# Twelve middle label slabs of a DLRM tower moved from VectorE to GpSimd and ScalarE

## The reference, cut to what matters

```python
score = exp((x @ w_a + b_a) @ w_b); p = softmax(where(mask == 0, PAD, score))
q     = einsum('bne,bn->be', x, p)                 # for two heads
h     = concat(q1, q2) @ w5 + b5
f7    = (h[:, iu] * h[:, ju] * g) @ w7 + b7
out8  = concat(h @ w6 + b6, f7) @ w8 + b8
z     = einsum('bu,bku->bk', out8, label_embedding)   # 1024 x 200 label rows of 300
y     = relu(relu(concat(z, ctx) @ W_top1 + b1) @ W_top2 + b2) @ W_top3
```

## Time and profile before

| what | value |
|---|---|
| median of 3 runs | 1833.36 us (1830.81 to 1834.02) |
| the profiled execution's own time | 1835.06 us |
| its span, first to last instruction | 1833.3 us |
| PE, DVE, ACT, POOL busy | 92%, 91%, 55%, 31% of the span |
| DMA, mean rate | 306 GB/s, 561.69 MB |
| mean granted clock of TensorE | 0.971 |

### The profile page before, as it was taken

The page is one execution under the profiler, slowest core; times in us unless marked ns, Lnnn a source line. Parts: engine busy times, 40 slices in busy tenths (PEclk is TensorE's granted clock), DMA queues, the critical chain, the costliest instruction groups (busy, mean ns, idle before and its releaser), DMA issues.

```text
span 1833.3 us, 25723 instructions
## 1 busy us (share of the span) xinstructions
PE 1686.3 (92%) x6972; PEld 1244.5 (68%) x6972; DVE 1661.9 (91%) x5847; ACT 1011.6 (55%) x3167; POOL 570.6 (31%) x419
## 2 busy tenths in 40 slices
PE   2888999999999999999999999999998999997754
PEld 1555667777767777777777777777775777775533
DVE  5988979989999889999999999899999788967777
ACT  3776693674466643466654664446753444354535
POOL 7778807828300135500077018600000000000044
PEclk8899999999999999999999999999999999999977
DMA  8388846847988689889868766998749999989987
GB/s 277 108 275 307 308 164 229 323 164 289 381 303 319 235 334 349 342 342 351 297 224 333 279 250 202 377 418 320 255 138 376 420 413 369 416 311 419 418 324 292
DMA packets 98222, 561.69 MB, mean 306 GB/s; under 512 B 16799, under 2 KB 17158, under 8 KB 72478
## 3 DMA queue, kind: packets, MB, share of 16 engines
q1 hardware_dynamic: 77917, 498.35, 70.5%
q0 software_dynamic: 19424, 61.65, 10.6%
q10 hardware_dynamic: 736, 0.05, 0.0%
HBM read 559.98 MB, written 0.00 MB: 305 GB/s over the span
## 4 chain that ended last, share of the span: by engine, by line
PE 42%; DVE 34%; DMA 10%; issue 6%; POOL 5%; ACT 2%; SPq 0%; DVEq 0%; POOLq 0%; ACTq 0%
PE acc L1132 37%; DVE qa L744 13%; DVE junk L700 12%; DVE prod L854 8%; DMA w_sb<-in_w 7%; POOL x L639 3%; DMA lab<-in_labels 2%; POOL lab L639 2%; ACT waste L1275 1%; PE coarse L938 1%; PE acc L985 1%; PE misc L950 1%; PE acc L988 1%; ACT prod L1380 1%; PE acc L970 1%
## 5 line engine op out<-in xcount | busy, mean ns | idle before, releaser
L1132 PE MATMUL acc<-w_sb,prod 128*128 128x300 f32 (+2 forms) x5648 | 1511.5, 421 | 59.8 <-DMA w_sb<-in_w 35.8
L1132 PEld LDWEIGHTS acc<-w_sb,prod 128*128 128x128 f32 (+2 forms) x5648 | 1052.8, 192 | 424.1 <-issue 48.6
L1380 ACT ACTIVATE prod<-prod,g_all 128x256 f32<-128x256 f32 (+4 forms) x1615 | 675.1, 470 | 475.9 <-DVE prod L854 471.2
L639 POOL DMA_INDIRECT x<-in_tbl,ids_sb x368 | 488.4, 1327 | 644.7 <-DVE qa L744 534.2
L854 DVE TENSOR_TENSOR prod<-fine,coarse 128x1280 f32<-128x1280 f32 (+3 forms) x320 | 419.5, 1316 | 93.1 <-PE coarse L938 72.3
L700 DVE SCALAR_TENSOR_TENSOR junk<-lab,heads 128x300 bf16<-128x300 f32 x1208 | 477.7, 462 | 10.9 <-DMA lab<-in_labels 9.6
L700 DVE SCALAR_TENSOR_TENSOR junk<-x,heads 128x300 bf16<-128x300 f32 x1128 | 445.4, 462 | 24.0 <-DMA x<-in_tbl,ids_sb 22.0
L744 DVE SCALAR_TENSOR_TENSOR qa<-x,ex,qa 128x300 f32<-128x300 f32 x612 | 275.7, 526 | 0.1
L674 POOL TENSOR_TENSOR x<-x,out 128x2400 f32<-128x2400 f32 x5 | 26.2, 5254 | 592.8 <-ACT out L1235 583.7
L1275 ACT ACTIVATE waste<-x 128x300 bf16<-128x300 f32 x368 | 161.7, 440 | 26.2 <-DMA x<-in_tbl,ids_sb 24.5
L1203 ACT ACTIVATE fine<-misc 128x512 f32<-128x512 f32 (+3 forms) x70 | 37.5, 535 | 116.9 <-PE misc L950 88.4
(11 more groups left out here) (123 smaller groups left out, 571.0 us busy)
## 6 DMA issues: line engine op xcount, KB each, us to landing
w_sb<-in_w SPq DMA_DIRECT2D x320, 750.0 KB, 6.7
lab<-in_labels SPq DMA_DIRECT2D x146, 1200.0 KB, 9.0
x<-in_labels SPq DMA_DIRECT2D x54, 1200.0 KB, 10.7
x<-in_tbl,ids_sb POOLq DMA_INDIRECT x368, 5.5
w_sb<-in_w SPq DMA_DIRECT2D x5, 450.0 KB, 3.3
prod<-in_v_i SPq DMA_DIRECT2D x1, 710.0 KB, 4.4
prod<-in_v_j SPq DMA_DIRECT2D x1, 710.0 KB, 5.8
w_sb<-in_w SPq DMA_DIRECT2D x1, 703.1 KB
```

The source lines that it names most:

```text
L639: pool.indirect_dma_start(out=row_of(t, n), out_offset=None, in_=tables[n], in_offset=bass.IndirectOffsetOnAxis(ap=ids_sb[:, t % IDS_RING, ...
L1132: last = pe.matmul(acc[:, t % 3, 0:EMB], prod[0:rows, u % RING, m, t % 2 * P:(t % 2 + 1) * P], w7_sb[0:rows, u % W7_RING, m * EMB:(m + 1) ...
L1380: act.activation(chunk, chunk, ACT.Copy, scale=g_all[0:rows, pair:pair + 1]).then_inc(chunk_ready, 1)
```

## The change

During the attention of tiles 4 to 7 the planner may give a label slab to POOL and ACT instead of DVE. It does so when a slab would be DVE's next item, the next item of `rest` is the `mask` of a tile t over 3, the slab is none of the first one or the last four of its label tile, the model says that all rows of t have landed, at least two `dots` items of t after the next are left, and POOL's last such multiplication is 60 (6 us by the model's clock) ago. DVE then takes the next item in its place at once. ACT's eight sums get a tick each from three units later on, in one sequence with the `sum_abs` rows, so that these move back; the slot is held to the last of the sums. POOL multiplies these slabs after the last gather of tile t and before the first of t + 1.

Followed through, the planner's arithmetic with its constants gives twelve such slabs: 11, 12, 14, 15 (labels of tile 0, beside the attention of tile 4; first sums at ticks 470, 493, 506, 524), 40, 43, 44 (tile 1, beside tile 5; 690, 698, 731), 69 (tile 2, beside tile 6; 895) and 84, 87, 88, 90 (tile 3, beside tile 7; 1050, 1058, 1091, 1104). All of DVE's other items keep their cost, but many change their unit. The `mask` of tile 4 stays at unit 111, that of tile 5 moves from 161 to 153, that of 6 stays at 191, that of 7 moves from 232 to 227. Up to the last unit of two tiles DVE ends its slabs at unit 280 instead of 283, tile 6's labels begin at unit 288 as before, and one slab more, 173, is done between the units (19 slabs of the tail are 18). `y` of tiles 1 and 3 comes 30 and 35 ticks later, that of 2 and 4 comes 30 and 15 ticks earlier.

The diff, cut to its core:

```diff
+POOL_COST = 60
@@ plan() @@
+    by_pool, pool_end = {}, 0
@@
         elif not (item and at <= now):
+            slab = None
             now = min(when for when in (1e9 if held else due, at, slab_at) if when > now)
             continue
+        if item == slab and c < TOTAL and rest and rest[0][0] == "mask" and 0 < slab[2] < SLABS - 4:
+            t = rest[0][1]
+            if (t > 3 and landed.get((t, HALVES - 1), 1e9) <= now and dots and dots[0][1] == t
+                    and dots[0][2] < HALVES - 2 and pool_end <= now):
+                pool_end = now + POOL_COST
+                for k in range(SLAB):
+                    abs_tick = max(abs_tick + 1, (u + 3) * FINE)
+                    pool_ticks.setdefault(abs_tick, []).append(("sum", nslab, k))
+                by_pool[nslab] = t
+                slab_end.append(now + (abs_tick - u * FINE) * UNIT[2] // FINE)
+                continue
@@ after plan() @@
+BEFORE, ITEMS, TAIL, POOL_TICKS, LOADS, SWITCH, MIDDLE = plan()
+SUMMED = {n: max(tick for tick, work in POOL_TICKS.items() if ("sum", n, SLAB - 1) in work) for n in MIDDLE}
-BY_POOL = [(TILES - 1) * SLABS + s for s in range(1, SLABS, 3)]
+BY_LAST = [(TILES - 1) * SLABS + s for s in range(1, SLABS, 3)]
+BY_POOL = list(MIDDLE) + BY_LAST
@@ schedule() @@
-        tick = (LABELLED.get(t, TOTAL) + 1) * FINE + 2
+        tick = max([(LABELLED.get(t, TOTAL) + 1) * FINE + 2] + [SUMMED[n] + 2 for n in MIDDLE if n // SLABS == t])
@@ POOL @@
+            def multiply(n):
+                pool.wait_ge(out8_ready, n // SLABS + 1)
+                slot, loads = slab_slot(n)
+                pool.wait_ge(slab_loaded[slot], 16 * loads)
+                row8 = out8[:, n // SLABS % OUT8, :]
+                row8 = bass.AP(tensor=row8.tensor, offset=row8.offset,
+                               ap=[list(row8.ap[0]), [0, SLAB], [1, EMB]])
+                pool.tensor_tensor(slab_place(slot), slab_place(slot), row8, ALU.mult).then_inc(multiplied, 1)
@@ POOL, for t in range(2, TILES), behind the gathers of t @@
+                for n in MIDDLE:
+                    if MIDDLE[n] == t:
+                        multiply(n)
@@ PE, turn_z @@
+                if sums_up_to(t):
+                    pe.wait_ge(sums_done, sums_up_to(t))
@@ ACT @@
+            def sum_row(slab, k):
+                t, column = slab // SLABS, slab % SLABS * SLAB + k
+                if k == 0:
+                    act.wait_ge(multiplied, BY_POOL.index(slab) + 1)
+                    if t >= Z_RING:
+                        act.wait_ge(y_stored, 16 * (t - Z_RING + 1))
+                slot, _ = slab_slot(slab)
+                product = slab_place(slot)[:, k, :]
+                act.activation(product, product, ACT.Copy,
+                               accum_out=z[:, t % Z_RING, column:column + 1]).then_inc(sums_done, 1)
@@ ACT, in the ticks @@
+                        elif name == "sum":
+                            sum_row(t, i)
```

More of the change, by code:

```diff
@@ L317, in plan @@
         loads.insert(at + 2 * n, load)
-    return before, items, tail, pool_ticks, loads, switch
-BEFORE, ITEMS, TAIL, POOL_TICKS, LOADS, SWITCH = plan()
+    return before, items, tail, pool_ticks, loads, switch, by_pool
+BEFORE, ITEMS, TAIL, POOL_TICKS, LOADS, SWITCH, MIDDLE = plan()
+SUMMED = {n: max(tick for tick, work in POOL_TICKS.items() if ("sum", n, SLAB - 1) in work) for n in MIDDLE}
 LABELLED = {item[1]: u for u in range(TOTAL) for item in ITEMS[u] if item[::2] == ("slab", SLABS - 1)}
-BY_POOL = [(TILES - 1) * SLABS + s for s in range(1, SLABS, 3)]
+BY_LAST = [(TILES - 1) * SLABS + s for s in range(1, SLABS, 3)]
+BY_POOL = list(MIDDLE) + BY_LAST
 TAIL = [(kind, t, s) for kind, t, s in TAIL if t * SLABS + s not in BY_POOL]
@@ L330, with sums_up_to @@
 FIRST_SLABS_OF_Z = -(-ZC // SLAB)
-FIRST_SUMS = sum(n % SLABS < FIRST_SLABS_OF_Z for n in BY_POOL)
+FIRST_SUMS = len(MIDDLE) + sum(n % SLABS < FIRST_SLABS_OF_Z for n in BY_LAST)
+def sums_up_to(t):
+    return SLAB * sum(n < (t + 1) * SLABS for n in BY_POOL)
 FIRST_Z_SUMS = SLAB * FIRST_SUMS
@@ L666, in _ @@
                     pool.wait_ge(gathered[t % 2][j], gathers(t))
[L667 to L674, removed]
+            for n in BY_LAST:
+                multiply(n)
         @block.vector
@@ L1276, in sum_abs @@
                                accum_out=absum[:, t % 2, n:n + 1]).then_inc(abs_done, 1)
+            def sum_row(slab, k):
[8 more added lines that the diff above has]
+                               accum_out=z[:, t % Z_RING, column:column + 1]).then_inc(sums_done, 1)
             def sum_rows(n):
-                act.wait_ge(multiplied, n + 1)
-                slot, _ = slab_slot(BY_POOL[n])
                 for k in range(SLAB):
[L1283 to L1286, removed]
+                    sum_row(BY_POOL[n], k)
             def exp_scores(t, fields=range(FIELDS)):
@@ L1395, in _ @@
             for name, of, n in END_BURSTS:
-                for summed in {"zt": range(2), "z_first": range(2, FIRST_SUMS),
+                for summed in {"zt": range(len(MIDDLE), len(MIDDLE) + 2), "z_first": range(len(MIDDLE) + 2, FIRST_SUMS),
                                "z_rest": range(FIRST_SUMS, len(BY_POOL))}.get(name, ()):
```

## The result

| | before | after |
|---|---|---|
| median | 1833.64 us (4 runs) | 1856.11 us (1851.92 to 1858.93, 4 runs) |
| ratio | | 1.012, interval 1.0108 to 1.0133 |
| the profiled execution's own time | 1835.06 us | 1851.92 us |
| its span | 1833.3 us | 1850.1 us |

A forecast was written before the change was run, and what follows sets the result against it. The prediction took PE's pace as the bound up to unit 283, then DMA bytes, then the last tile's chain. Terms +1 - 2 - 2.5 - 0.5 - 0.4 + 2.9 gave -1.5 us: 1831.9 us as median, range 1821 to 1842.

The forecast's parts named there:

- The picture of the bounds: Whole kernel: PE bounds up to unit 283, DMA bytes from 288 to 324, then the last tile's chain.
- The collision of `pooled` with POOL's product: Unit 91, tile 4: `pooled` of tile 3 falls into slab 11's multiplication; taken as 1 us, between 0 and 2.9.
- Late slots: Unit 148: slab 48's load, waiting for ACT's sums of slab 44, might cost DVE its lead; tile 5's end of +3.
- rival B: Late products and late slots (tick 1050, slots of 44 and 88) become units' last wait; about 1843 us, chance 0.23.
- The term of tile 4: Units 88 to 112: later DVE blocks and items plus the collision, less 1.3; +1 us, ends -1.3 and +4.
- Tile 5: Units 133 to 175: `wsums` start at 155, spread among slabs, instead of back to back; -2 us, ends -2.5 and +3.
- Units 176 to 190: Tile 6's gathers end earlier, easing unit 180's `w7` wait and clock fall; -2.5 us, between 0 and -4.2.
- Units 205 to 213: Tile 7: +2 for ACT waiting on POOL, -2.5 for fewer loads before `w7`; -0.5 us, ends -4 and +4.
- Units 226 to 283: Same DVE items two slabs on, same loads before each `w7`; -0.4 us, ends -2 and +3.
- The end: Units 288 to the last: one more label load, slab 182, before the last `w7`; +2.9 us, ends 0 and 3.5.
- small gains: Forecast gains: -1.3 within tile 4's stretch, -2 at tile 5, -2.5 at units 176 to 190 and for tile 7's loads.

The follow-up runs named there:

- e4: Changed kernel with the load of slab 182 moved behind the last `w7` on SP; median 1856.6 us, ratio 1.0124.
- e1: Changed kernel with POOL waiting for `pooled` of the tile before ahead of its middle products; median 1848.01 us, ratio 1.0074.
- m11: Changed kernel with POOL's wait for `pooled` of tile 3 ahead of its second product (slab 12) only; median 1848.31 us, ratio 1.0082.
- m9: k8 without POOL's wait for `pooled` ahead of the middle products; median 1841.35 us, ratio 1.0039.
- e2: Changed kernel without its four middle slabs beside tile 4 (11, 12, 14, 15), eight left; median 1842.48 us, ratio 1.0048.
- m12: e1 with the planner putting ACT's sums ahead of `sum_abs` beside tile 4 only, ten slabs; median 1837.67 us, ratio 1.0027.
- e3: Changed kernel with slab 84 multiplied behind the 35th gather of tile 7 instead of behind all 50; median 1856.9 us, ratio 1.0121.
- k7: Changed kernel with the edits of e1, e3 and e4 together; median 1841.04 us, ratio 1.0039.
- k8: e1 with the planner giving sums the earliest ticks (ten slabs), slab 85's product behind the 35th gather, slab 182 behind the last `w7`; 1826.73 us, ratio 0.9958.

## Why the prediction was wrong

The picture of the bounds held: PE's pace, DMA bytes at the end, no gain from 37 us less on DVE in itself. What failed is the price of the new waits, nearly all on one side.

- **The collision of `pooled` with POOL's product** was priced at 1 us between 0 and 2.9. It cost 6.6 us by unit 93 of the changed kernel's profile, 11.8 in e4's, and 8.1 in the medians (e1). Two things were wrong in it. The lower half of the range was taken although the cited section of the Trainium skill speaks for the upper end: that page's rule, that the two exclude one another for a whole instruction, is what m11 shows. And the upper end itself counted the one product that was running, when three stood in POOL's queue with their data landed; "a whole instruction" was read as the whole wait. With the fall of the clock, which was not in the term either, one shut-out came to 10 us (m9).
- **Late slots** had a price in the prediction at unit 148 alone, as an end of +3; rival B named the slot of 88, without one. The change has the same risk wherever `sum_abs` and sums share a sequence: beside tile 4 (20.9 us of waits on DVE, some 4 us of PE's in e1 against e2) and tile 7 (14.5 us of waits; 4 to 6 us of the time by m12). The term of tile 4 said +1 and was +9.4; e1's +5.3 is what it was without the collision. That the gathers of tiles 4 and 5 end 20 us before the first sum, which stood against rival B, speaks of products and not of when ACT lets the slot go.
- **Tile 5**, -2 forecast, was +3.1 from unit 113 to 175. The 82 ticks without a free one were noticed for tile 4, but only as load on ACT; that the mask of tile 5, now eight units earlier, has to wait for the end of its own sequence of `sum_abs` rows and sums (4.5 us in the changed kernel, 0.3 before) was not asked. What part of the 3.1 us is this wait isn't shown.
- **Units 176 to 190**, -2.5 forecast, gave -4.4 by unit 182, with the clock at 1.00: right in kind, just beyond its end.
- **Units 205 to 213**, -0.5 forecast (+2 for ACT's wait, -2.5 for fewer loads), came to +2.7. The step that failed is that of the loads. It counted how many stand before `w7` of unit 211, whose wait went as forecast; it did not ask which stand directly before `w7` of unit 210, where two took the place of one. PE's wait there was 3.64 us for 0.45, and unit 209 took 9.51 us for 6.32. At unit 210 nearly all the gain was then lost to the clock: 8.13 us before, 6.03 in e3 and k7, and 7.71 in the changed kernel. ACT's wait came where it was forecast (2.75 us, against 3.8), but it didn't end last, so it isn't shown that it cost anything.
- **Units 190 to 205** had no term, and 2.8 us were lost between 182 and 205. e3 and k7 lose them too, so they aren't the product's; their cause stays open.
- **Units 226 to 283**, -0.4 forecast, measured +0.5 (215 to 284). The number came out by luck: PE lost 2.9 us to unit 237, where late slots held DVE, and won 2.4 back up to 284.
- **The end**, +2.9, measured +3.1 at unit 323 and +3.8 at `out8`: right in kind and nearly in size, though it is slab 181, now ahead of `w7` of unit 323, that shows at 323. e4's edit gave 2 of it back.

Rival B named the right kind of cause, late products and late slots, with its places (the slots of 44 and 88, unit 91), gave 1843 and had 0.23. At tick 1050 the late product that it counted on was there, but `w7` came later still. Its price was short by several products at once and by slots beside tile 4. The sum of parts also let small gains (-1.3, -2, -2.5) stand against bounded losses as if both were as sure. In k8's plan, where little else comes late, the kernel did gain, 0.4%.

## What to carry to other kernels

Before work is moved from a busy engine to idle ones, list for each moved piece who waits for its end: the buffer it holds, the queue behind it, and the instruction beside it. Here such waits outweighed all that twelve slabs off DVE gave. A long GpSimd operation on SBUF goes where DVE has nothing with two SBUF inputs, or behind a wait for the last such; that wait gave 8 us in one plan and 15 in another. And when a shared engine must serve both a buffer's release and a due date, let the planner place both with their real order: twelve slabs in one order were 1.2% slower, ten in another, with the wait and the two other fixes, 0.4% faster. And count for each late load what stands directly ahead of it in the queue, not only how many loads the stretch has.

## What the runs showed of the hardware

DVE's addition with both inputs in SBUF (`pooled`, 128x600, 0.77 us) took 3.37 us beside one GpSimd product of 5.30 us, 8.5 us in three profiles and 13.74 us in one where three products followed each other without a gap. GpSimd's next instruction can thus go ahead of a DVE instruction that has long waited, once or twice, and the number isn't the same in each run. The Trainium skill ("SBUF — State Buffer", section "SBUF: two separate sides") tells of an exclusive hold for a whole instruction; the single product agrees with it, and the queue of products is worse than a reader takes from it. DVE's `cross`, with one input in PSUM (1.49 us beside a product, 1.49 alone), and its rows (0.46 us both ways, `heads` being in PSUM too) were not touched, which agrees with that page's section "Who interferes with whom".
